# Last layer's attention: scores of two steps issued together, projections beside the transposes, a loop body of eight head pairs

## The reference

```python
def _L3_attn_ref(x, Wq, Wk, Wv, Wo, bo, rel_pos_bias):      # 16 heads of 64
    B, T, _ = x.shape
    q = (x @ Wq).reshape(B, T, H, dh).transpose(0, 2, 1, 3)
    ...                                                      # k, v likewise
    logits = jnp.einsum('bhqd,bhkd->bhqk', q, k)
    logits = logits + causal[None, None] + _pos_bias(rel_pos_bias, T)[None]
    logits = logits / dh
    probs = jax.nn.softmax(logits, axis=-1)
    out = jnp.einsum('bhqk,bhkd->bhqd', probs, v)
    out = out.transpose(0, 2, 1, 3).reshape(B, T, H * dh)
    return out @ Wo + bo
```

## Time and profile before

| | us |
|---|---|
| median of 3 runs | 4982.19 |
| lowest, highest run | 4964.53, 5005.42 |
| the profiled execution | 5000.41 |
| its span, first to last instruction | 4998.4 |

### The profile page before, as it was taken

How to read it: one execution, slowest core, us unless ns; L and a number is a source line. 1 busy time by engine, 2 the same in 40 slices (tenths; PEclk the granted TensorE clock), 3 DMA queues, 4 the chain that set the end, 5 groups by cost and what they waited for, 6 DMA issues and landing times. The chain is left out here.

```text
span 4998.4 us, 110868 instructions
## 1 busy us (share of the span) xinstructions
PE 3769.8 (75%) x37428; PEld 2195.0 (44%) x37428; DVE 2816.7 (56%) x7044; ACT 2049.2 (41%) x4247; POOL 999.6 (20%) x1324
## 2 busy tenths in 40 slices
PE   4699999749975999735999943455447339999998
PEld 1244444337752222123666621135446226666665
DVE  5577777641134888655555554843543355555554
ACT  4366666513333677612222212221102125555553
POOL 0000000000000000002666530600001514444441
PEclk9799999859986999957999966566558669999999
DMA  3322111100002211000000001010000413333331
GB/s 99 66 51 50 49 48 48 30 9 10 9 1 63 44 43 39 20 4 11 15 15 15 15 23 40 32 55 29 4 4 2 49 64 111 110 109 109 110 110 33
DMA packets 179786, 218.22 MB, mean 44 GB/s; under 512 B 36509, under 2 KB 154852, under 8 KB 179182
## 3 DMA queue, kind: packets, MB, share of 16 engines
q1 hardware_dynamic: 175470, 206.76, 14.4%
q0 software_dynamic: 4096, 8.40, 1.1%
HBM read 162.16 MB, written 34.60 MB: 39 GB/s over the span
## 5 line engine op out<-in xcount | busy, mean ns | idle before, releaser
L628 ACT ACTIVATE att_E<-att_pX,att_gs 128x512 f32<-128x512 f32 (+3 forms) x1536 | 844.9, 580 | 416.5 <-PE att_pX L565 288.3
L659 DVE TENSOR_REDUCE att_mx<-att_pS 128x1 f32<-128x512 f32 (+3 forms) x1536 | 812.4, 546 | 202.5 <-PE att_pS L547 136.3
L545 PE MATMUL att_pS<-att_ks,att_qs 72*128 72x512 bf16 (+4 forms) x1536 | 524.0, 342 | 116.6 <-DVE att_mx L659 51.7
L563 PE MATMUL att_pX<-att_qs,att_ks 75*128 75x512 bf16 (+4 forms) x1536 | 507.6, 332 | 55.8 <-ACT att_E L628 54.8
L1789 POOL TENSOR_TENSOR att_E<-att_E,att_rz 128x128 f32<-128x128 f32 (+3 forms) x512 | 357.5, 719 | 465.9 <-DVE att_rz L1995 465.9
L545 PEld LDWEIGHTS att_pS<-att_ks,att_qs 76*128 76x128 bf16 (+1 forms) x1536 | 149.3, 97 | 575.0 <-DVE att_mx L659 480.3
L1482 POOL TENSOR_TENSOR pairs_h<-pairs_c,pairs_r 128x512 f32<-128x512 f32 x272 | 344.8, 1270 | 191.4 <-DVE pairs_c L1542 190.5
L1529 ACT ACTIVATE pairs_r<-pairs_ph 128x512 f32<-128x512 f32 x272 | 162.4, 597 | 438.7 <-PE pairs_pc L1500 435.8
L1542 DVE TENSOR_TENSOR pairs_c<-pairs_pc,pairs_r 128x512 f32<-128x512 f32 x272 | 188.1, 692 | 254.8 <-ACT pairs_r L1529 253.9
L576 PE MATMUL att_pO<-att_E,att_vs 128*9 128x512 f32 (+3 forms) x3072 | 323.6, 493 | 1.6 <-ACT att_E L628 1.6
L1927 ACT ACTIVATE att_E<-att_S,att_nm 128x128 f32<-128x128 f32 (+3 forms) x512 | 281.5, 552 | 80.9 <-DVE att_nm L1989 80.8
(11 more groups left out here) (421 smaller groups left out, 6912.9 us busy)
## 6 DMA issues: line engine op xcount, KB each, us to landing
att_bias<-in_bias_dram SPq DMA_DIRECT2D x64, 896.0 KB, 4.4
parts<-proj_part SPq DMA_DIRECT2D x144, 128.0 KB, 2.3
att_xb<-xnT SPq DMA_DIRECT2D x64, 256.0 KB, 2.6
att_qs<-parts SPq DMA_DIRECT2D x192, 64.0 KB
att_ks<-parts SPq DMA_DIRECT2D x192, 64.0 KB
att_w<-in_w3a_dram SPq DMA_DIRECT2D x64, 192.0 KB, 2.4
att_qs<-parts SPq DMA_DIRECT2D x96, 96.0 KB
att_ks<-parts SPq DMA_DIRECT2D x96, 96.0 KB
```

The lines of the kernel that those rows point to most:

```text
L545: ins = nc.tensor.matmul(pS[:, r % 2, :w], qs[:K1, u, x, j * P:(j + 1) * P], ks[:K1, u, x, :w], start=True, stop=not causal)
L563: ins = nc.tensor.matmul(pX[:, s % 2, :w], ks[:, g % NB, x, kt * P:(kt + 1) * P], qs[:, g % NB, x, q0(kt):], start=True, stop=not causal)
L628: nc.scalar.activation(E[:, kt % 2, x, :w], pX[:, s % 2, :w], ACT.Exp, scale=gs[:, g % 2, x // maps:x // maps + 1]).then_inc(s_e, 1)
L659: V.reduce_max(mx[:, h % NB, r:r + 1], pS[:, r % 2, :w1(r % QT)], AX.X).then_inc(s_mx, 1)
```

## The change

On PE, `AHEAD` becomes 4, and at j = 0 and j = 2 the scores of two steps, s + 4 and s + 5, are issued one after the other; j = 1 and j = 3 issue none. `through_wo` of the last pair goes from j = 1 to j = 0, behind these scores; v of the next pair to j = 1, q and k of the pair after it to j = 2 and j = 3; each now stands directly before the transposes. On ACT, `leave` follows: v at j = 1, q at j = 2, k at j = 3, before the exponentials of that step. On DVE `add` goes to j = 0, behind the extremes, with a drain before it; the inversions and POOL's divisions run three steps ahead instead of two. The body is eight pairs (one batch) on every engine and runs 8 times instead of 32; with this the batch and pair indices of the loads and of wo are constants in the body. The counts in `at(...)` follow.

```diff
-    ROWS = 2 * IR
-    STEPS = 2 * QT
+    ROWS = PAIRS * IR
+    STEPS = PAIRS * QT
-    AHEAD = 3
+    AHEAD = 4
...
                     for s in range(STEPS):                      # PE
                         m, j = divmod(s, QT)
-                        if j == 0 and not (last and m == 1):
-                            project(at, 1, m + 1, first)
-                        if j == 1 and not (first and m == 0):
-                            through_wo(at, i, m - 1, not (last and m == 1))
-                        if not (last and s + AHEAD >= STEPS):
+                        if j % 2 == 0 and not (last and s + AHEAD >= STEPS):
                             scores(at, s + AHEAD, first)
+                            scores(at, s + AHEAD + 1, first)
+                        if j == 0 and not (first and m == 0):
+                            through_wo(at, m - 1, not (last and m + 1 >= PAIRS))
+                        if j == 1 and not (last and m + 1 >= PAIRS):
+                            project(at, 2, m + 1, first)
+                        if j >= 2 and not (last and m + 2 >= PAIRS):
+                            project(at, j - 2, m + 2, first)
                         if not (last and s + 1 >= STEPS):
                             turn(at, 2 * s + 2, first)
                             turn(at, 2 * s + 3, first)
-                        if j == 2 and not (last and m == 1):
-                            project(at, 2, m + 1, first)
-                        if j == 3 and not last:
-                            project(at, 0, m + 2, first)
                         weigh(at, s, first)
...
                         if j == 0 and not (first and m == 0):   # ACT
                             outputs(at, m - 1, first and m == 1)
-                        if j == 0 and not (last and m == 1):
-                            leave(at, 1, m + 1, first)
+                        if j == 1 and not (last and m + 1 >= PAIRS):
+                            leave(at, 2, m + 1, first)
+                        if j >= 2 and not (last and m + 2 >= PAIRS):
+                            leave(at, j - 2, m + 2, first)
...
-                def add(at, i, m):                              # DVE
-                    b = (i * 2 + m) // PAIRS
+                def add(at, b, m):
                     dst = R.s[:, bass.ds(b * QT, QT), :].rearrange("p q d -> p (q d)")
-                    dve.wait_ge(s_y, at(2, m + 1))
+                    dve.drain()
+                    dve.wait_ge(s_y, at(PAIRS, m + 1))
...
-                        if not (last and s + 2 >= STEPS):
-                            invert(at, s + 2, first)
-                        if j == 1 and not (first and m == 0):
-                            add(at, i, m - 1)
+                        if not (last and s + 3 >= STEPS):
+                            invert(at, s + 3, first)
                         if not (last and s + AHEAD >= STEPS):
                             extreme(at, 2 * (s + AHEAD), first)
                             extreme(at, 2 * (s + AHEAD) + 1, first)
+                        if j == 0 and not (first and m == 0):
+                            add(at, i if m else i - 1, m - 1)
```

More of the change, by code:

```diff
@@ L1768, in body @@
                     at = At(sp, i)
[L1769 to L1779, removed]
+                    for m in range(PAIRS):
+                        u = m % 2
+                        begin = first and m < 2
+                        if not begin:
+                            sp.wait_ge(s_pr, at(3 * PAIRS, 3 * m - 3))
+                        sp.dma_start(w[:, u].rearrange("p k f -> p (k f)"), t["w3a"][m]).then_inc(s_w[u], 16)
+                        sp.dma_start(xb[:, u], R.xnT[:, bass.ds(i * T, T)]).then_inc(s_w[u], 16)
+                        if not begin:
+                            sp.wait_ge(s_mx, at(ROWS, IR * (m - 1)))
+                        sp.dma_start(bias[:, u], t["bias3"][:, m, :]).then_inc(s_b[u], 16)
+                run_bodies(sp, B, body)
             @block.gpsimd
@@ L1948, in body @@
                         leave(at, 0, 1, True)
+                        leave(at, 1, 1, True)
                         for r in range(2 * AHEAD):
@@ L1959, in body @@
                                 copy(at, r, first)
-                        if j == 2 and not (last and m == 1):
-                            leave(at, 2, m + 1, first)
-                        if j == 3 and not last:
-                            leave(at, 0, m + 2, first)
                         if not (last and s + AHEAD >= STEPS):
@@ L1967, in body @@
                     if last:
-                        outputs(at, 1, False)
-                run_bodies(act, COUNT, body)
+                        outputs(at, PAIRS - 1, False)
+                run_bodies(act, B, body)
             @block.vector
@@ L2015, in body @@
                             extreme(at, r, True)
-                        invert(at, 0, True)
-                        invert(at, 1, True)
+                        for t_ in range(3):
+                            invert(at, t_, True)
                         copy(at, 0, True)
@@ L2032, in body @@
                     if last:
-                        dve.drain()
-                        add(at, i, 1)
-                run_bodies(dve, COUNT, body)
+                        add(at, i, PAIRS - 1)
+                run_bodies(dve, B, body)
 H2, HK, HV, C = 4, 32, 64, 32
```

52 lines of the change are left out of this document (25 added, 27 removed).

## The result

| | before | after the change |
|---|---|---|
| median us (20 runs each) | 4988.25 | 5007.94 |
| lowest, highest | 4964.53, 5013.59 | 4991.03, 5022.47 |
| span of the profiled execution | 4998.4 | 5018.7 |
| the stage, from the start of the first projection to that of the last addition | 816.8 | 836.0 |

A forecast was written before the change was run, and what follows sets the result against it. TensorE, 99.8% busy in the last layer's attention, was taken as the bound. Per pair -0.30 + 0.43 + 0.26 = +0.39 us, some 24 us, took the median from 4,982.2 to 5,006; own range 4,995 to 5,018, over the cases 4,956 to 5,036.

The forecast's parts named there:

- The sum of a steady pair: Net effect per head pair in the last layer's attention: -0.30 saved, +0.43 and +0.26 waits, giving +0.39 us.
- The jumps: Branches back at the end of the attention loop's bodies: 24 fewer of them, taken as worth 0.
- First new wait, wo: PE at `through_wo`, moved behind two short scores groups, waits for ScalarE's `outputs`: 0.43 us a pair.
- The chain I summed to 3.81: From k's start through ScalarE's leave, two exponentials and `outputs` until wo resumes: 3.81 us, against 3.38 of PE work.
- Second new wait, v: PE's v projection waits for VectorE's `add` to free bank `pA`: 2.15 us from wo against 1.89, wait 0.26.
- VectorE starts 0.24 later: Term in v's wait: delay from the end of wo's matmuls to VectorE's addition, 0.24 us.
- bodies of eight pairs: I take 0: Longer loop body, run 8 times instead of 32: the 24 branches saved show no worth, taken as 0.
- Scores behind scores: Two scores groups in a row on PE, twice a pair: a further saving of 0 to 0.20 us, taken as 0.
- Shapes: Array shape changes on PE: groups left for another shape fall from ten to eight a pair, 0.20 us saved.
- Instruction fetch: Rival at the loop's five jumps back: longer bodies fetched anew, 10 to 20 us more, 5,016 to 5,026; chance 0.12.
- no new stall: Rival for the attention loop: 0.30 to 0.50 us a pair saved, neither wait, 4,950 to 4,963 us; chance 0.16.

The follow-up runs named there:

- e7: e6 with ScalarE's `outputs` between the two exponentials of 512 columns instead of behind both: 4996.68 against 4996.51 us before the change, ratio 1.0005.
- e8: e6 with scores issued one step at a time, never behind scores: single run, 5056.93 us beside 4996.51 before the change.
- e1: The change's order with loop bodies of two pairs on every engine, indices back in registers: 4983.78 against 4964.34 us before the change, ratio 1.0041.
- e10: e9 with `outputs` placed as in e7 and VectorE's addition ahead of the inversion and extremes: 4952.73 against 4991.33 us before the change, ratio 0.9926.
- e11: e10 with v's projection behind the six transposes instead of ahead of them: 4940.27 against 4991.33 us before the change, ratio 0.9907.
- e3: The change's order with a body of eight pairs on PE only, two on the other engines: single run, 4995.11 us beside 4964.34 before the change.
- e4: The change's order with a body of two pairs on PE, eight on the other engines: single run, 4977.68 us beside 4964.34 before the change.
- e5: The change with 54 small matmuls (216 PE instructions) ahead of its loop: single run, 5025.37 us beside 4996.51 before the change, added matmuls included.
- e6: The change without three implied PE waits a pair, PE's body 1,703 instructions: 5012.55 against 4996.51 us before the change, ratio 1.0031.
- e9: e6 with four-pair bodies on engines other than PE, addition's batch index computed once per body: 4986.71 against 4991.33 us before the change, ratio 0.9997.

## Why the prediction came out right, and where it was not

**The time: right, by two errors that offset each other.** Forecast +24 us, measured +20. The sum of a steady pair was +0.39 and measured -0.14, over some 62 pairs 33 us too slow. The jumps were at nothing in the sum and measured 25 us. That the two nearly cancel is luck; agreement of the total says little about its terms.

**First new wait, wo: shown.** Forecast 0.43; PE's row has 0.47, and against PE's own 3.15 from k to wo (e7; I had 3.38) the wait is 0.54. And e7 and e8 show that it is ScalarE's queue: with `outputs` one exponential earlier the wait is gone, with less PE work ahead of wo the stretch from k keeps its length. The chain I summed to 3.81; e1, with register indices as before, has 3.84, and the change 3.69. The agreement with e1 is in part luck: ScalarE starts the leave 0.04 us after k's end in both, not 0.12, and wo resumes 0.19 after `outputs` in e1, not 0.06.

**Second new wait, v: mis-sized.** Forecast 2.15 from wo to v and a wait of 0.26. e1 has 2.13, the change 1.95; the wait is some 0.06. The term that failed is "VectorE starts 0.24 later". I took it from an extreme behind scores in the kernel before, where register work lies behind the wait. Without it the addition starts 0.04 after wo's end. So the sentence "bodies of eight pairs: I take 0" was the failing step twice over: it overlooked the register work that the long body takes from behind the two waits (-0.15 and -0.18 a pair), and the fetches.

**Scores behind scores: free, where I took the bound.** 384 and 512 keys take 1.70 together, not 0.84 + 1.06: the 0.20 that I left in the range is a gain on the path. The like gain at 128 and 256 keys (0.85 for 1.06) disappears in wo's wait. With the 0.12 of wo's chain and the 0.20 of v's, this is the 0.52 between the forecast 12.94 and 12.41.

**Shapes: as read.** k to transposes is 0.96, as said, and likewise for q; the leave prices of the earlier trace rows carried over.

**Instruction fetch: the rival named it and I gave it 0.12.** Its size was 10 to 20 us, the measured one 25.0. I had counted about 1,750 instructions on PE (1,720 it is), and wrote "the queue moves nothing in the steady part now" against it. That was no argument: it showed that two pairs stay resident, and nothing about four times as many. The stops of the earlier trace rows, 1.5 and 2.1 us, were the right kind of row but too small a price, since those are of code that runs straight on; a jump took 3.46 us on PE. The stop was not PE's alone. And I priced a stop by its length: that the granted clock is 0.50 for 3.4 to 6.8 us behind it, 9.6 of the 25.0 us, was in no term.

**Faster than before was left out of the middle.** The rival "no new stall" said 4,950 to 4,963; e10 and e11, which take both waits away (e10 all but 0.17 us at v in half the pairs), land at 0.9926 and 0.9907 of before. That case was real, but not for the order as changed.

## What to carry to other kernels

Where an order puts a wait on the path, price the chain with the form that its instructions will have (here an instruction with register work behind its wait started 0.14 to 0.19 us later), and look at what stands ahead of the producer in its own queue: moving `outputs` ahead of one exponential and the addition ahead of one inversion turned a loss into a gain of 1%. Unroll a loop only as far as every engine's body stays resident, and decide that from the packets of the instruction queues, one engine at a time. Price a stop of TensorE with the slower clock behind it: here 15.4 us of standing cost 25.0. When a total agrees with a forecast, still look at the distances one by one: here an average of 12.9 was made of 12.41 and 17.

## What the runs showed of the hardware that I had not expected

- A loop of 1,720 instructions on PE was fetched anew on each turn (56 packets, 3.46 us of stop); the same loop, 216 instructions further on, was not (12 packets, no such stop; a single run). Bodies of 1,711 and 1,703 were not either. What the limit is in terms of where the blocks begin stays open.
- VectorE's and ScalarE's bodies of 452 and 381 instructions were fetched anew (60 to 64 packets, stops of 1.3 to 3.9 us); 230 and 193 were not (3 packets).
- The stops overlap: PE's alone made 24.5 us, the others' alone 12.5, all together 25.0.
- Behind a stop of PE the granted clock was 0.50 (1.2 GHz) for 3.4 or 6.8 us: at all five jumps in the change, at four in e3, one in e4, three in e5 and in e6, five in e8, none in e9. It made 9.6 of the 25.0 us.
- A second group of scores right behind a first takes 0.20 us less than one after another shape (384 and 512 keys: 1.70 for 0.84 + 1.06).
- Register work behind a satisfied wait showed as 0.14 us on PE (0.19 for 0.05) and 0.19 us on VectorE (0.23 for 0.04).
